# Moving the work between two expert layers into the copied code paths, and holding the second layer's up weights in memory

## What is computed

```python
x = x + _L0_ffn_ref(_layernorm(x), ...)      # 8 experts, 704 wide, top 2, and a shared one
h = jnp.einsum('bld,ed->ble', rmsnorm(x), W_in) + b_in          # third step ("wi")
x = x + depool + h
scores = jax.nn.sigmoid(x @ gate_w.T)                            # 32 experts, 8 groups of 4
masked = jnp.where(best 4 of the groups, scores + e_bias, 0)
topk_w = scores of the best 6, over their sum, times 2.5
h = jnp.square(jax.nn.relu(jnp.einsum('th,eih->tei', x, up_w)))  # 256 -> 128
moe = jnp.einsum('tei,ehi->th', h * combine, down_w)             # 128 -> 256
shared = relu2(x @ shared_up_w.T) @ shared_down_w.T              # 256 -> 512 -> 256
x = x + moe + shared
```

## Time and profile before

| what | value |
|---|---|
| runs, median of 3 | 803.28 us |
| the profiled execution: its own time | 802.19 us |
| its span, first to last instruction | 800.4 us |
| PE busy | 718.6 us (90%) |
| DVE busy | 400.3 us (50%) |
| ACT busy | 274.3 us (34%) |
| POOL busy | 309.3 us (39%) |
| mean granted TensorE clock | 0.931 |
| HBM traffic | 261 GB/s over the span |

### The profile page before, as it was taken

One profiled execution on the slowest core, in us unless ns is written; L12 is line 12 of the kernel. 1 busy time (PEld: TensorE's weight loads), 2 busy tenths in 40 slices (PEclk: granted clock), 3 DMA queues, 4 the chain that ended last, 5 costly groups with the idle time before them and its releaser, 6 DMA issues.

```text
span 800.4 us, 14611 instructions
## 1 busy us (share of the span) xinstructions
PE 718.6 (90%) x4686; PEld 638.6 (80%) x4686; DVE 400.3 (50%) x1522; ACT 274.3 (34%) x604; POOL 309.3 (39%) x328
## 2 busy tenths in 40 slices
PE   4898998999999999999999999689892999969766
PEld 3687787899999999999999989556561899858654
DVE  4988977522333333544765365338421444435453
ACT  2643542222111111123232313123430777736440
POOL 1322330670001111001155317603765577777660
PEclk9877895999999999999999999959996999989998
DMA  8999993237767676756686762513556999999996
GB/s 247 401 296 266 261 266 102 88 107 243 229 216 243 208 225 227 259 168 207 217 286 245 253 209 108 199 45 95 178 176 188 330 353 360 315 373 382 390 322 240
DMA packets 109946, 190.59 MB, mean 238 GB/s; under 512 B 11681, under 2 KB 75766, under 8 KB 109726
## 3 DMA queue, kind: packets, MB, share of 16 engines
q1 hardware_dynamic: 94464, 148.06, 58.6%
q0 software_dynamic: 13344, 38.68, 12.7%
q10 hardware_dynamic: 2046, 2.71, 1.1%
HBM read 143.46 MB, written 65.62 MB: 261 GB/s over the span
## 4 chain that ended last, share of the span: by engine, by line
PE 68%; DVE 10%; DMA 8%; issue 5%; POOL 5%; ACT 2%; SPq 1%; POOLq 0%; DVEq 0%; ACTq 0%
PE PB L579 22%; PE PB L617 14%; PE PB L593 5%; PE PB L776 4%; PE PB L785 4%; DMA MEM<-in_w 3%; POOL rows_in L1820 3%; POOL rows_out L1859 2%; PE PB L502 2%; PE PB L733 2%; PE PB L644 2%; PE PB L764 2%; DMA X<-in_x 2%; PE PB L561 1%; DMA rows_out<-WS,MEM 1%
## 5 line engine op out<-in xcount | busy, mean ns | idle before, releaser
L579 PE MATMUL PB<-XT,MEM 128*128 128x128 f32 x1584 | 186.6, 277 | 0.3 <-issue 0.3
L579 PEld LDWEIGHTS PB<-XT,MEM 128*128 128x128 f32 x1584 | 182.4, 193 | 0.6 <-issue 0.5
L1811 POOL DMA_INDIRECT sorted_y<-WK x36 | 34.5, 959 | 242.4 <-DVE WK L1433 241.5
L1820 POOL DMA_INDIRECT rows_in<-MEM x96 | 93.2, 971 | 60.8 <-DVE MEM L1622 32.3
L617 PE MATMUL PB<-MEM,WK 128*128 x432 | 99.5, 380 | 0.0
L617 PEld LDWEIGHTS PB<-MEM,WK 128*128 128x128 f32 x432 | 79.4, 190 | 9.6 <-issue 0.2
L776 PE MATMUL PB<-MEM 128*128 128x128 f32 x456 | 64.9, 288 | 14.7 <-DMA MEM<-in_w 13.4
L776 PEld LDWEIGHTS PB<-MEM 128*128 128x128 f32 x456 | 59.1, 203 | 17.1 <-issue 11.6
L1859 POOL DMA_INDIRECT rows_out<-WS,MEM x58 | 57.4, 990 | 32.2 <-ACT WS L996 16.3
L892 ACT ACTIVATE XT<-PB 128x256 f32<-128x256 f32 x52 | 19.9, 382 | 142.7 <-PE PB L561 142.7
L1748 DVE TENSOR_TENSOR WK<-WK,PB 128x256 f32<-128x256 f32 x57 | 24.0, 421 | 79.6 <-ACT WK L1007 79.4
(11 more groups left out here) (274 smaller groups left out, 1193.8 us busy)
## 6 DMA issues: line engine op xcount, KB each, us to landing
MEM<-in_w SPq DMA_DIRECT2D x36, 896.0 KB, 7.1
rows_in<-in_consts SPq DMA_DIRECT2D x32, 600.0 KB, 12.1
MEM<-in_w SPq DMA_DIRECT2D x148, 128.0 KB, 2.3
MEM<-in_w SPq DMA_DIRECT2D x36, 512.0 KB, 3.8
MEM<-rows_in SPq DMA_DIRECT2D x58, 300.0 KB, 5.2
MEM<-rows_out SPq DMA_DIRECT2D x16, 768.0 KB, 7.8
MEM<-in_w SPq DMA_DIRECT2D x2, 3072.0 KB, 19.6
sorted_x<-MEM SPq DMA_DIRECT2D x1, 5070.0 KB, 38.9
```

The costliest lines, as they stand in the source:

```text
L579: t = e.matmul(o[:, to:to + P], UPW[m][i % (3 - m)][:, k, c * P:(c + 1) * P], XT[:, n % 2, k, :], start=(k == 0), stop=(k == 1))
L1811: e.indirect_dma_start(out=DY, out_offset=bass.IndirectOffsetOnAxis(ap=DEST[:, i:i + 1], axis=0), in_=YS[:, i % 2, :], in_offset=None).the ...
L1820: e.indirect_dma_start(out=DX1, out_offset=bass.IndirectOffsetOnAxis(ap=SLOT1[:, i, j:j + 1], axis=0), in_=XR[:, i, :], in_offset=None).th ...
```

## The change

1. **The copies are longer.** `after_blocks` is called at the end of `end0` in each program, so the mid work and the units stand in each of the five copies, and the jump out of a copy comes after the last unit (for POOL, after group 3's scatters).
2. **Another order.** Group 2's steps from `t1` on are placed for each number of pages (`EXTRA`); in this run `t1` and `wi` stay at iterations 49 and 50, and `t2` goes into iteration 51. `BEHIND` is a list for each number of pages: the sums of group 3 stand ahead of group 2's `ro`, and group 2's `rank` behind group 3's `t1`. `pages_left` is a step of its own ("left"), and the page numbers ("pages") are worked out behind unit 8.
3. **Up weights in memory.** `W1E` holds up and down weights of all 32 experts (256 KB an expert in each load in place of 128 KB). SP's `weights2` is gone. DVE's `weights2(s)` copies the two experts' up weights of a pair into `WUP[s % 4]`, three pairs ahead; PE waits for `bw` in place of `wu`.

```diff
@@ -235,22 +231,32 @@
 
 READY = tuple(8 * g + 15 for g in range(NR - 1))
 GATHER = {READY[g] + 2: g for g in range(NR - 1)}
-STEPS = {}
+NAMES = "sum", "t1", "wi", "t2", "ro", "rank"
+STEP_AT = 0, 1, 2, 4, 5, 6
+STEPS, EXTRA, BEHIND = {}, {}, {}
 for g_ in range(NR - 1):
-    for k_, at_ in enumerate((0, 1, 2, 4, 5, 6)):
-        if g_ < 2 or k_ < 3:
+    for k_, at_ in enumerate(STEP_AT):
+        if g_ < 2 or k_ == 0:
             STEPS.setdefault(READY[g_] + 3 + at_, []).append((g_, k_))
-BEHIND = ("t2", 2), 0, ("ro", 2), ("sum", 3), 1, 2, ("rank", 2), 3, ("q1", 3), ("t1", 3), 4, ("wi", 3), 5, 6, (
-    "q2", 3), ("t2", 3), 7, ("ro", 3), 8, ("rank", 3), *range(9, 16), 16
-NAMES = "sum", "t1", "wi", "t2", "ro", "rank"
+for nb_ in BLOCKS:
+    k_ = 1
+    for i_ in range(BLOCKS[0], nb_ + LATE):
+        if k_ < 6 and (i_ >= nb_ or i_ - READY[2] - 3 >= STEP_AT[k_]):
+            EXTRA[nb_, i_] = [(2, k_)]
+            k_ += 1
+    rest_ = [(name, 2) for name in NAMES[k_:]]
+    BEHIND[nb_] = [*rest_[:-2], ("sum", 3), *rest_[-2:-1], 0, 1, 2, ("q1", 3), ("t1", 3), *rest_[-1:], 3, ("wi", 3), 4,
+                   *([("left", 2)] if rest_ else []), 5, ("q2", 3), ("t2", 3), 6, ("ro", 3), 7, ("rank", 3), ("left", 3),
+                   8, ("pages", 3), *range(9, 17)]
 
 
 def steps_of(n, nb):
-    return STEPS.get(n - EARLY, ())
-
-
-def after_blocks(mid, up1, down1):
-    for what in BEHIND:
+    i = n - EARLY
+    return EXTRA.get((nb, i), ()) if i >= BLOCKS[0] else STEPS.get(i, ())
+
+
+def after_blocks(nb, mid, up1, down1):
+    for what in BEHIND[nb]:
         if isinstance(what, tuple):
             mid(what[1], what[0])
             continue
...
         YS = WK[:, 0:512].rearrange("p (a d) -> p a d", a=2)
-        W1E = MEM[:, 0:E1 * 256].rearrange("p (e c) -> p e c", e=E1)
-        W1U = MEM[:, 9216:11264].rearrange("p (a b c) -> p a b c", a=4, b=2)
+        W1E = MEM[:, 0:E1 * 512].rearrange("p (e c) -> p e c", e=E1)
         W1S = MEM[:, 16384:16384 + SC * 512].rearrange("p (e c) -> p e c", e=SC)
...
+        WUP = [m[:, a + 512 * k:a + 512 * k + 512].rearrange("p (b c) -> p b c", b=2)
+               for m, a in ((WK, 3116), (MEM, 18432)) for k in range(2)]
         D2 = WK[:, 3628:3628 + P]
...
                     busy[b7] = ("counted", g)
+                if name == "pages":
+                    q.wait_ge("d2")
+                    q.wait_ge("set1", "ones")
+                    idle(3)
+                    e.matmul(PB[:, 3, 0:P], ONF, D2, start=True, stop=True).then_inc(*q.mark("pages"))
 
             def block_iteration(n, nb):
...
+                    if g == 0:
+                        idle(4)
+                        idle(5)
                 for t4 in range(m):
...
 
-            after_blocks(mid, up1, down1)
-            q.wait_ge("d2")
-            q.wait_ge("set1", "ones")
-            idle(3)
-            e.matmul(PB[:, 3, 0:P], ONF, D2, start=True, stop=True).then_inc(*q.mark("pages"))
+            busy0 = dict(busy)
+
+            def end0(c):
+                nb = BLOCKS[c]
+                busy.clear()
+                busy.update(busy0)
+                for n in range(SPLIT, EARLY + nb + LATE + 1):
+                    block_iteration(n, nb)
+                    down(n - 1, nb)
+                q.wait_ge("done0")
+                after_blocks(nb, mid, up1, down1)
+
+            q.copies(number, BLOCKS, end0)
             q.wait_ge("pgs")
             number1 = e.value_load(PAGES, min_val=0, max_val=P)
...
                 q.wait_ge("bh", s - 4)
                 q.wait_ge("ebk")
                 q.wait_ge("drn", NR - 1)
                 for j in range(2):
                     for k in range(2):
-                        t = e.matmul(PB[:, 4 + s % 4, j * P:(j + 1) * P], W1U[:, s % 4, j, k * P:(k + 1) * P],
+                        t = e.matmul(PB[:, 4 + s % 4, j * P:(j + 1) * P], WUP[s % 4][:, j, k * P:(k + 1) * P],
                                      XTB[:, s % 3, j, k, :], start=(k == 0), stop=(k == 1))
                 t.then_inc(*q.mark("bu", s))
...
                 q.wait_ge("bh", s)
                 q.wait_ge("by", s - 2)
                 for j in range(2):
-                    w = W1E[:, bass.ds(expert(packed, 2 * s + j), 1), :].rearrange("p e c -> p (e c)")
+                    w = W1E[:, bass.ds(expert(packed, 2 * s + j), 1), 256:512].rearrange("p e c -> p (e c)")
...
                     if s % 2 == 0:
                         if s == 0:
-                            q.wait_ge("tabe")
...
 
-            def end0(c):
-                nb = BLOCKS[c]
-                del means[started:]
-                for n in range(SPLIT, EARLY + nb + LATE + 1):
-                    block_iteration(n, nb)
-                    result(n - 1, nb)
-                    left(n, nb)
-                q.wait_ge("done0")
-
-            started = len(means)
-            q.copies(number, BLOCKS, end0)
...
             def behind_blocks(g, name):
                 mid(g, name)
-                if name == "rank":
+                if name == "left":
                     pages_left(g)
+                    if g == NR - 1:
+                        number_pages()
+                if name == "pages":
+                    page_experts()
+
+            def number_pages():
+                q.wait_ge("base", NR - 1)
+                e.tensor_scalar(D2, ident, EV[:, 4:5], None, ALU.mult).then_inc(*q.mark("d2"))
+
+            def page_experts():
+                q.wait_ge("pages")
+                e.tensor_copy(EBK, PB[:, 3, 0:P]).then_inc(*q.mark("ebk"))
+                e4, pack = EBK[0:1, :].rearrange("p (q j) -> p q j", j=4), OVER[0:1, :]
+                q.wait_ge("ebk")
+                e.scalar_tensor_tensor(pack, e4[:, :, 3], float(E1), e4[:, :, 2], ALU.mult, ALU.add).then_inc(*q.mark("l1_v"))
+                for j in (1, 0):
+                    q.wait_ge(*q.last)
+                    e.scalar_tensor_tensor(pack, pack, float(E1), e4[:, :, j], ALU.mult, ALU.add).then_inc(*q.mark("l1_v"))
+                q.wait_ge(*q.last)
+                e.tensor_copy(TABE[:, 0:32], pack).then_inc(*q.mark("tabe"))
+                e.tensor_copy(PAGES, EV[0:1, 1:2]).then_inc(*q.mark("pgs"))
 
             def down1(n):
                 c, g = UNITS[n]
...
+            def end0(c):
+                nb = BLOCKS[c]
+                del means[started:]
+                for n in range(SPLIT, EARLY + nb + LATE + 1):
+                    block_iteration(n, nb)
+                    result(n - 1, nb)
+                    left(n, nb)
+                q.wait_ge("done0")
+                after_blocks(nb, behind_blocks, lambda n: None, down1)
+
+            started = len(means)
+            q.copies(number, BLOCKS, end0)
...
 
+            def weights2(s):
+                q.wait_ge("bu", s - 4)
+                for j in range(2):
+                    t = e.tensor_copy(WUP[s % 4][:, j, :], W1E[:, bass.ds(expert(packed, 2 * s + j), 1), 0:256].rearrange(
+                        "p e c -> p (e c)"))
+                t.then_inc(*q.mark("bw", s))
+
             def sum_rows(i):
                 y = Y6[place(i)]
...
             def step(s, n_pairs):
+                if s < 0:
+                    q.wait_ge("tabe")
+                    for j in range(4):
+                        q.wait_ge(f"w1{j}", 8 * j + 7)
+                for k in range(0 if s < 0 else s + 3, min(s + 4, n_pairs)):
+                    if k % 2 == 0:
+                        packed[k // 2] = four_experts(q, k // 2)
+                    weights2(k)
                 if s + 1 < n_pairs and (s + 1) % 2 == 0:
                     meta1((s + 1) // 2)
                 if 0 <= s < n_pairs:
...
                         rows_out(1, min(5 * (nb - READY[1] - 9), 24), 24)
+                for g in range(2, NR):
+                    rows_out(g, 0, 24)
 
             q.copies(number, BLOCKS, end0)
-            for g in range(2, NR):
-                rows_out(g, 0, 24)
             q.wait_ge("pgs")
...
+                    e.dma_start(W1E[:, k, :], w1[SC + k]).then_inc(*q.land(f"w1{k // 8}", k))
+
+            def up1(n):
+                load_expert("u1", n)
+                load_expert("u1", n)
 
             def end0(c):
                 nb = BLOCKS[c]
...
 
             q.copies(number, BLOCKS, end0)
-
-            def up1(n):
-                load_expert("u1", n)
-                load_expert("u1", n)
-
-            after_blocks(lambda g, k: None, up1, lambda n: None)
             q.wait_ge("pgs")
...
-            packed = {}
-
-            def weights2(s):
-                q.wait_ge("tabe")
-                if s // 2 not in packed:
-                    packed[s // 2] = four_experts(q, s // 2)
-                q.wait_ge("bu", s - 4)
-                for j in range(2):
-                    e.dma_start(W1U[:, s % 4, j, :],
-                                w1[bass.ds(expert(packed, 2 * s + j) + SC, 1), :, 0:256].rearrange("e p c -> p (e c)")
```

(6 more changed lines are left out.)

54 lines of the change are left out of this document (12 added, 42 removed).

## The result

| | before | changed |
|---|---|---|
| median of 4 runs each | 802.06 us (800.84 to 804.39) | 779.49 us (779.04 to 786.09) |
| ratio | | 0.973, 95% interval 0.968 to 0.979 |
| the profiled execution, its span | 802.19, 800.4 us | 779.04, 777.2 us |
| the same in a later comparison (11 and 6 runs) | 799.65 us | 783.55 us, ratio 0.979 (0.974 to 0.983) |

The account below looks back on a forecast made before the run. POOL's scatters were taken as the bound, late in the front and through the pairs. Terms -15.6 (front), +1.0 (jump), -4.0 (up weights), +4.0 (copies) sum to -14.6 us from 803.28: 788.7 us, range 780 to 802.

Parts of the forecast that it names:

- the front: Stretch from the first layer's last block to the second layer's first pair; forecast to end 15.6 us earlier.
- No jump: Before the mid work: moving the jump away removes TensorE's two issue gaps, 5.8 us; group 2's `t2` costs 1.1 us.
- Group 3's sums ahead: DVE does group 3's sums before group 2's picks; with the jump moved, POOL starts group 2 12.6 us earlier.
- Group 3's slots: Between POOL's two groups: the 3.33 us wait for group 3's slots falls to the normal 0.30, 3.0 us gained.
- Page numbers inside units: Behind unit 8 TensorE stands 4.6 us for DVE's left pages and its clock drops; covered before the pairs' rows come.
- Jump now: The jump behind the last shared unit, ahead of the pairs, on TensorE and DVE: 1.0 us lost.
- Up weights: 114 up-weight DMAs go, 4.0 us of POOL's waits gained in the pairs; larger expert loads cost nothing.
- Copies: DVE's two copies a pair lengthen POOL scatters that start in them, 0.035 us a copy: 4.0 us lost.
- tail: Landing, fetching and summing after the last scatter, 22.8 us, left unchanged.
- rival 2: The front gives less: low TensorE clock, or pauses reaching beyond 603.3, make pairs start 4 to 5 us later; 795; chance 0.12.
- rival 4: Group 3's slots come over 1 us after POOL finishes group 2, each us costing one; 792; chance 0.03.
- The floor of 779.3: Lowest time: the front's 15.6 us plus all 8.4 us of POOL's loss in the pairs gained, nothing lost at the jump.

Follow-up runs that it names:

- e3: The changed kernel with the old order of group 2's and group 3's steps, all inside the longer copies; 788.4 us, ratio 0.985 to the kernel before.
- e1: The changed kernel with up weights fetched by two DMAs a pair again, 128 KB expert loads and no DVE copies; 793.2 us, ratio 0.990 to the kernel before.
- e2: The kernel before with only the third part, up weights in memory and two copies a pair; 791.3 us against 801.0, ratio 0.989.
- e10: The changed kernel as it is, run and traced a second time; ratio 0.979 to the kernel before.
- e7: The changed kernel with each pair's two up-weight copies made twice, 228 copies in all; ratio 0.980 to the kernel before.
- e4: The changed kernel with up weights copied for the first four pairs only, leaving later results wrong; ratio 0.978 to the kernel before.
- e8: The changed kernel with SP's first six fetches of the pairs' rows inside the copies, ahead of SP's jump; ratio 0.979 to the kernel before.
- e9: The changed kernel with three expert loads a unit, and SP's first six fetches and DVE's first three pairs' copies ahead of the jump; 781.1 us, ratio 0.977.

## Why the prediction was right and wrong

The direction and the mechanism of the front were right; the sum was 4.9 us short of the 19.5 that the stages give. By its steps:

| step | forecast | measured |
|---|---|---|
| *No jump* and *Group 3's sums ahead*: group 2 starts earlier | -12.6 | -12.6 (A) |
| *Group 3's slots* | -3.0 | -2.0 (B) |
| *Page numbers inside units* | covered | covered |
| *Jump now* | +1.0 | +0.3 |
| *Up weights*: the expert loads, "cost them at nothing" | 0 | +1.9 (the rest of C; not shown to be theirs) |
| *Up weights*: POOL's waits | -4.0 | -4.8 (D) |
| *Copies* | +4.0 | +0.5, and 2.2 less by the sums' share (D) |
| tail | 0 | -0.6 (E) |
| sum | -14.6 | -19.5 |

- **Front.** The 12.6 came true to the decimal, which flatters it. The traces put A no closer than 1.5 us. Its inner split was off: e3 shows 8 to 9.6 for the jump (gaps and clock) and 3.0 for the order, and DVE's last result was not delayed by the `t2` in iteration 51 (6.7 us behind the last `sorted_y` scatter, 7.5 before). The clock was low from 515 to 518 and again from 529 to 532 (0.50 to 0.6), else 1.00: rival 2 named a real thing of smaller size.
- **Group 3's slots.** The prediction gave 49.7 us from the start of the sums to the slots; it was 51.9. POOL waited 1.37 for them in place of 0.30: rival 4, at its threshold.
- **Page numbers.** TensorE stood 4.59 us (forecast 4.6) and then worked at 0.50 for some 5 us; it ended its units at 596.4 (598 forecast). Here is the row of the pause, and the clock behind it:

```profile
567.46 0.80 PE L692 MATMUL PB<-WK,MEM 128*128 128x128 f32 x2 [4.59 <-DVE WK L1678]
```

```profile
569.00:571.00 2.00, 2.00 (x4) 0.91 (x3) 0.63 (x4) 0.00 (x0) 1.39 (x3) 0.50 0.24 94
```

- **Jump now.** The step looked at TensorE and DVE only. SP jumps as well, for 4.5 us right behind its last load, and the pairs' first fetch stands behind that jump in its queue; SP does not occur in the step. Yet SP's jump costs 0.3 us and the two others' nothing, as the table of the handover shows. The other 1.9 us of C are the later landing of POOL's last scatter and of the second pair's rows, while the expert loads are in flight. The prediction put these loads at nothing by a DMA share of 0.64, a mean over 52 us; from 588 to 592 us, ahead of the last scatter, the share is 0.94 in the changed kernel. That the first pair's rows came at 602.9 where 603.3 was forecast is luck: the start gave 3.7 us, and the stages A and B took 1.1 and the handover 2.2 more than forecast.
- **Up weights.** Right in kind: waits of TensorE for `wu` went, and POOL's with them, nearly all of the 4.9 instead of 4.0. e1 and e2 show it both ways.
- **Copies.** This step failed, and it is the largest error, 3.5 us. From the earlier trace rows the prediction read that a scatter ends late by what the DVE operation has left *less 0.13*, and then priced the copies at their whole remaining time, 0.15 on average. With the 0.13 taken off, a copy of 0.29 costs at most 0.16, and on average 0.16 x 0.16 / 2 / 0.29 = 0.04 for the 0.23 of them that meet a start: 1.2 us for 114. Measured: 0.5 (0.3 in e10, 2.1 for the 228 of e7).
- **The sums' share.** That it would fall from 3.7 to 1.5 was in no step. Both traces of the changed kernel have it (1.5, 1.4); in the other kernels without `wu` it is 2.0 to 3.6 (e2, e3, e4, e7, e8, e9). It looks like how the phases of sums and scatters fall in each kernel, rather than an effect of the change; no run shows it.
- **Ranges and rivals.** The floor of 779.3 assumed all of POOL's 8.4 us gone and a free jump. Most of the distance from 782.6 (802.06 - 19.5) to the 779.5 measured is the start's spread, which the range had no term for: the runs of before that were shown spread by 3.5 us, and that should have widened it at both ends.

## What to carry to other kernels

A jump out of a long copied path leaves gaps of 3.4 us on TensorE (and 2.5 more shortly behind), 3.6 on DVE up to its first copy and 4.5 on SP here, and costs nothing where another engine ends later: ahead of the mid work it cost 8 to 9.6 us, ahead of the pairs 0.3. Before you move first issues ahead of a jump, check in the chain what they wait for: e8 did so and gained nothing, since the landing of the last scatter was what ended late. When a stage gets faster, what was covered by it (SP's DMA issues, jumps) must be added to the sum again. A row that gives a rule with a constant in it (remaining time less 0.13) must be used with the constant, above all for operations not much longer than it.

## What the runs showed of the hardware

- An indirect DMA on POOL that starts while a sum of two SBUF operands or a copy (128x256 f32, SBUF to SBUF) runs on DVE takes longer by the operation's remaining time less 0.13 us (0.10 for 0.23 left, 0.66 for 0.78 left); operations that start inside it add nothing. A product with one operand in PSUM doesn't hold it (L1778 with 0.37 left at 633.14 in the changed kernel: 0.96).
- The granted clock from 60 to 100 us was 0.83 in one execution of the changed kernel and 0.74 in another (e10), and over all traces 0.74 to 0.87 with the same code up to there; the scatter at 138 us moves by 5 us with it.
- Two pauses of 3.4 and 2.5 us behind a jump cost TensorE's clock for 14 us behind them (0.50 from 522 to 536): to move the jump away gave 7.9 to 9.6 us, where the pauses are 5.8.
- POOL's last scatter of `rows_in` landed 2.6 to 2.9 us after its start in the kernel before, e3 and e9, and 3.6 to 4.3 in the changed kernel, e10, e4, e7 and e8, where SP's 256 KB loads were in flight beside it.
- In one stretch of time all kernels took 100 us more, with pauses of 0.3 to 2.4 us between matmuls that wait for nothing the profile shows.
